# Pre stage run inside the local-attention loop, with keys and values stored by column modulo 4

## What is computed

```python
h = _L0_tok_ref(x, ...)                      # attention in 8x8 windows
h = h + _L0_attn_ref(_layernorm(h), ...)     # local attention: the stage of the change
h = h + _L0_ffn_ref(_layernorm(h), ...)      # routed experts
h = h + _L1_attn_ref(_layernorm(h), ...)     # linear attention with decay
h = h + _L1_ffn_ref(_layernorm(h), ...)      # binary weights behind a gate

def local_mask(seq_len, window_size=7):      # queries see keys at most 3 rows and 3 columns away
    ok_row = jnp.abs(row[:, None] - row[None, :]) <= half
    ok_col = jnp.abs(col[:, None] - col[None, :]) <= half
    return ok_row & ok_col
qkv = (x @ W_qkv.T).reshape(Bb, Nn, 3, NUM_HEADS, HEAD_DIM)
attn = jnp.einsum('bhqd,bhkd->bhqk', q, k) * (scale * temperature[0])
attn = jax.nn.softmax(jnp.where(mask, attn, -jnp.inf), axis=-1)
out = jnp.einsum('bhqk,bhkd->bhqd', attn, v) @ W_proj.T + b_proj
```

## Time and profile before

| | us |
|---|---|
| median of 3 runs | 1976.49 |
| lowest, highest | 1973.61, 1978.38 |
| the profiled execution's own time | 1986.12 |
| its span, first to last instruction | 1984.3 |
| PE busy in the span | 1697.9 (86%) |
| DVE, ACT, POOL busy | 1182.7, 975.5, 422.9 |
| mean granted TensorE clock (share of full speed) | 0.955 |

### The profile page before, as it was taken

How to read it: one execution, slowest core, us unless ns; L and a number is a source line. 1 busy time by engine, 2 the same in 40 slices (tenths; PEclk the granted TensorE clock), 3 DMA queues, 4 the chain that set the end, 5 groups by cost and what they waited for, 6 DMA issues and landing times.

```text
span 1984.3 us, 94332 instructions
## 1 busy us (share of the span) xinstructions
PE 1697.9 (86%) x35690; PEld 1234.3 (62%) x35690; DVE 1182.7 (60%) x3445; ACT 975.5 (49%) x1765; POOL 422.9 (21%) x477
## 2 busy tenths in 40 slices
PE   5999999956568888888888779999999999999996
PEld 3566666644457666666667556666666666666663
DVE  2565656567624444444444467777777777777762
ACT  2344444423312222222222227777777777777776
POOL 2100000034322332323323222222222222222210
PEclk9899999978979999999999969999999999999998
DMA  3100000125533333333333212333333333333332
GB/s 106 36 11 13 11 11 13 32 57 104 102 86 93 92 96 94 93 96 91 97 96 92 63 33 74 79 79 79 79 79 79 79 79 79 79 79 79 79 78 57
DMA packets 254173, 141.71 MB, mean 71 GB/s; under 512 B 181314, under 2 KB 218050, under 8 KB 253858
## 3 DMA queue, kind: packets, MB, share of 16 engines
q1 hardware_dynamic: 254114, 140.88, 29.5%
HBM read 63.56 MB, written 18.42 MB: 41 GB/s over the span
## 4 chain that ended last, share of the span: by engine, by line
issue 33%; PE 29%; SPq 26%; ACT 6%; DVE 2%; DMA 2%; POOL 1%; ACTq 0%; DVEq 0%; POOLq 0%
SPq L402 13%; PE ps_D L805 8%; SPq L391 4%; ACT prob L1060 3%; PE ps_AV L822 3%; SPq L373 2%; PE ps_J L859 2%; PE ps_J L911 2%; PE ps_OT L929 2%; PE ps_J L879 2%; SPq L428 1%; PE ps_J L937 1%; PE ps_OT L954 1%; SPq L394 1%; PE ps_OT L953 1%
## 5 line engine op out<-in xcount | busy, mean ns | idle before, releaser
L1060 ACT ACTIVATE prob<-ps_D 128x1024 bf16<-128x1024 f32 x448 | 443.6, 1022 | 83.6 <-PE ps_D L805 83.2
L1231 DVE TENSOR_REDUCE m_sb<-ps_D 128x4 f32<-128x400 f32 x256 | 135.4, 571 | 207.7 <-PE ps_D L708 192.1
L1048 ACT ACTIVATE prob<-ps_D 100x512 f32<-100x512 f32 x256 | 139.0, 595 | 216.8 <-PE ps_D L730 216.8
L493 POOL TENSOR_TENSOR tile_a<-q_st,q_mask 128x1024 f32<-128x1024 f32 x64 | 123.3, 1927 | 407.5 <-DMA q_st<-q_d 369.5
L730 PE MATMUL ps_D<-tile_a,key_patch 64*100 64x128 f32 x2048 | 176.7, 288 | 0.0
L726 PE MATMUL ps_D<-mT,key_rows 64*100 64x128 bf16 x1024 | 129.3, 224 | 51.0 <-ACT mT L1037 32.2
L1184 DVE TENSOR_REDUCE top<-ps_D 128x8 f32<-128x512 f32 x128 | 79.5, 684 | 152.5 <-PE ps_D L582 152.5
L805 PE MATMUL ps_D<-tile_b,w_parts 128*128 128x256 bf16 x1024 | 155.5, 275 | 15.5 <-ACT prob L1060 9.6
L805 PE MATMUL ps_D<-tile_a,w_parts 128*128 128x256 bf16 x1024 | 156.1, 276 | 14.2 <-ACT prob L1060 9.6
L730 PEld LDWEIGHTS ps_D<-tile_a,key_patch 64*100 64x100 f32 x2048 | 146.8, 166 | 0.0
L805 PEld LDWEIGHTS ps_D<-tile_a,w_parts 128*128 128x128 bf16 x1024 | 88.5, 100 | 60.3 <-issue 47.8
(11 more groups left out here) (174 smaller groups left out, 3880.9 us busy)
## 6 DMA issues: line engine op xcount, KB each, us to landing
tile_b<-v_d SPq DMA_DIRECT2D x640, 40.0 KB
tile_a<-xg SPq DMA_DIRECT2D x384, 64.0 KB, 2.0
tile_b<-xg SPq DMA_DIRECT2D x384, 64.0 KB, 2.0
key_st<-k_d SPq DMA_DIRECT2D x64, 175.0 KB, 3.0
key_st<-k_d SPq DMA_DIRECT2D x64, 167.0 KB, 3.1
w_exp<-experts SPq DMA_DIRECT2D x64, 129.0 KB, 2.3
k_d<-kpad SPq DMA_DIRECT2D x32, 140.0 KB, 2.3
xin<-in_x SPq DMA_DIRECT2D x32, 128.0 KB, 2.3
```

The costliest lines, as they stand in the source:

```text
L493: gp.tensor_tensor(q_block[:, par, :].rearrange("c (p h q) -> c p h q", h=NH, q=NQ), q_st[:, :].rearrange("c (p a q) -> c p a q", a=1, q=N ...
L1048: act.activation(prob1[0:NKL, 2 * g + x, :], s_loc[x][0:NKL, :], ACT.Exp).then_inc(T2["exp_done"], 1)
L1060: act.activation(sgn[:, k % 4, :], unit(k, par)[:, :], ACT.Sign).then_inc(BN["sign"], 1)
L1231: dve.tensor_reduce(m_sb[:, C * x + HOT[x] + 4 * g:C * x + HOT[x] + 4 * g + 4], m_loc[x][:, 0:4 * NKL].rearrange("p (u n) -> p u n", u=4), ...
```

## The change

The pre stage loses its own loop. It now works by strips of 256 tokens (64 instead of 32 turns of half the size), and its strip `m = i + 5` (`LEAD = 5`) is worked in the same turn as local strip `i`, on PE, ACT and DVE; moments and normalization (DVE, POOL) are for `i + 6`. Five strips of it run alone ahead of the loop. SP has one loop, too: in the turn of strip `i` it loads the edge rows of `i`, waits until pre strip `i + 2` is stored, loads keys and queries of `i + 1`, loads the values of `i`, and stores pre strip `i + 3`.

In `k_d` and `v_d` a row is now four groups of 18 columns, one for each column modulo 4 (`NC = 18`, `ROW = 72`; before, 70 columns in order). The columns of one offset for the 16 patches then lie together in `v_d`, so values come in four transfers of 30, 30, 20 and 20 partitions with 4096 bytes each. The keys of a patch have a new order (`key_order`), applied in the host's tables and in two copies on POOL instead of one.

```diff
             def store_rows(b, s, m, par):
-                sp.wait_ge(L["k_sb"], times(i + 1))
+                sp.wait_ge(L["k_sb"], times(m + 1))
...
-                for y in range(2):
-                    dst = v_d[bass.ds(b, 1), bass.ds((w * WIN + HALF + y) * PW, 7 * PW), :].rearrange("a n c -> (a n) c")
-                    sp.dma_start(bass.AP(dst.tensor, dst.offset + HALF * C, [[C, W], [2 * PW * C, 4], [1, C]]),
-                                 v_sb[C * y:C * (y + 1), par, :, :]).then_inc(L["stored%d" % par], 16)
+                for t in range(2):
+                    dst = v_d[bass.ds(b, 1), bass.ds((s * QP + HALF + 2 * t) * ROW, 2 * ROW), :].rearrange("a n c -> (a n) c")
+                    sp.dma_start(bass.AP(dst.tensor, dst.offset + C, [[NC * C, 2 * QP], [C, W // QP], [1, C]]),
+                                 v_sb[:, par, t, :]).then_inc(L["stored%d" % par], 16)
...
+            def values_in(b, s, i, par):
                 sp.wait_ge(T2["av_done"], credited((i - 1) * 2))
                 settle(sp)
-                for r in range(KS):
-                    src = v_d[bass.ds(b, 1), bass.ds((s * QP + r) * PW, PW), :].rearrange("a n c -> (a n) c")
-                    sp.dma_start(v_patch[r * KS:(r + 1) * KS, par, :, :], bass.AP(src.tensor, src.offset, [[C, KS], [QP * C, 16], [1, C]])).then_inc(T2["v_in%d" % par], 16)
+                for column, first, steps in ((1, 0, 3), (2, 0, 3), (0, 1, 2), (3, 0, 2)):
+                    src = v_d[bass.ds(b, 1), bass.ds(s * (QP * ROW) + column * NC + first, NC), :].rearrange("a n c -> (a n) c")
+                    sp.dma_start(v_patch[at:at + KS * steps, par, :, :].rearrange("k a c -> k (a c)"),
+                                 bass.AP(src.tensor, src.offset, [[ROW * C, KS], [C, steps], [1, (W // QP) * C]])).then_inc(T2["v_in%d" % par], 16)
...
+            def strip_io(b, s, pair, par):
+                i = b * STRIPS + s
+                edge_in(s, i, par)
+                stored(b * (STRIPS // 2) + pair + 1, par)
+                keys_in(b, s + 1, i + 1)
+                values_in(b, s, i, par)
+                store_rows(b, s + 3, i + 3, 1 - par)
```

(of `strip_io` the cases at the ends are left out). POOL and PE in a strip:

```diff
-                gp.tensor_copy(key_patch[:, par, :].rearrange("c (p r w) -> c p r w", p=8, r=KS), patches(key_st)).then_inc(T2["k_patch"], 1)
+                keys = key_patch[:, par, :].rearrange("c (p n) -> c p n", p=8)
+                gp.tensor_copy(keys[:, :, 0:6 * KS].rearrange("c p (b r w) -> c p b r w", b=2, r=KS), patches(key_st, NC, NC, 3)).then_inc(T2["k_patch"], 1)
+                gp.tensor_copy(keys[:, :, 6 * KS:10 * KS].rearrange("c p (b r w) -> c p b r w", b=2, r=KS), patches(key_st, 1, 3 * NC - 1, 2)).then_inc(T2["k_patch"], 1)
...
                 scores(j, par, 0)
+                if not last:
+                    peak(*after(j, par), 0)
+                if m is not None:
+                    pre_turn(m)
                 if not first:
-                    project(i - 1)
+                    project(i - 1, min(i + LEAD, NS) if isinstance(i, int) else i + LEAD)
+                if m is not None:
+                    pre_values(m, 1 - par)
                 scores(j, par, 1)
                 if not last:
-                    peak(*after(j, par), 0)
+                    peak(*after(j, par), 1)
                 values(j, par, 0)
+                if m is not None:
+                    pre_keys(m, 1 - par, i)
                 if not last:
-                    peak(*after(j, par), 1)
+                    turn_maxima(i + 1, made(j, par))
                 values(j, par, 1)
-                if not last:
-                    turn_maxima(i + 1)
```

More of the change, by code:

```diff
@@ L43, in head_rows, with key_order @@
     return r // 32, r % 32 // HD, r % HD
+def key_order():
+    order = []
+    for b, steps in ((1, (0, 1, 2)), (2, (0, 1, 2)), (0, (1, 2)), (3, (0, 1))):
+        order += [r * KS + QP * step + b - 1 for r in range(KS) for step in steps]
+    return order
 def shape_tables():
@@ L286, in strips_ahead, with ahead, made @@
             strip(0, 1)
-            with eng.Fori(1, NSTRIP // 2 - 1) as j:
+            full = (NSTRIP - LEAD - 1) // 2
+            with eng.Fori(1, full) as j:
                 strip(j, 0)
                 strip(j, 1)
-            strip(NSTRIP // 2 - 1, 0)
-            strip(NSTRIP // 2 - 1, 1)
+            for j in range(full, NSTRIP // 2):
+                strip(j, 0)
+                strip(j, 1)
+        def ahead(j, par):
+            i = j * 2 + par
+            m = i + LEAD
+            return m if not isinstance(i, int) or m < NSTRIP else None
+        def made(j, par):
+            i = j * 2 + par
+            return min(i + LEAD + 1, NSTRIP) if isinstance(i, int) else i + LEAD + 1
         def pairs(eng, part, end=1):
@@ new lines, in image @@
+            def image(b):
+                with sp.Fori(0, STRIPS // 2 - 2) as pair:
+                    strip_io(b, pair * 2, pair, 0)
+                    strip_io(b, pair * 2 + 1, pair, 1)
+                for pair in (STRIPS // 2 - 2, STRIPS // 2 - 1):
+                    strip_io(b, pair * 2, pair, 0)
+                    strip_io(b, pair * 2 + 1, pair, 1)
+            sp.wait_ge(T1["av_done"], times(NT))
+            store_rows(0, 0, 0, 0)
+            store_rows(0, 1, 1, 1)
+            sp.wait_ge(L["padded"], times(16 * 6 * B))
@@ L409, in _ @@
+            stored(0, 0)
+            stored(0, 1)
+            keys_in(0, 0, 0)
+            store_rows(0, 2, 2, 0)
+            with sp.Fori(0, B - 1) as b:
+                image(b)
+            image(B - 1)
             sp.wait_ge(s_prep, 2)
@@ L1043, in strip, with weights @@
                 i = j * 2 + par
-                for g in range(2):
+                m = ahead(j, par)
+                def weights(g):
                     act.wait_ge(T2["scores"], credited(i * 2 + g + 1))
@@ L1251, in strip @@
                 i = j * 2 + par
+                m = ahead(j, par)
+                nxt = made(j, par)
+                more = not isinstance(nxt, int) or nxt < NS
                 first, last = isinstance(i, int) and i == 0, isinstance(i, int) and i == NS - 1
+                if not last:
+                    maxima(i + 1, 0)
                 if not first:
                     residual(i - 1)
+                if more:
+                    pre_moments(nxt)
                 if not last:
-                    maxima(i + 1, 0)
                     maxima(i + 1, 1)
+                if m is not None:
+                    pre_queries(m, j + 2 + par, 1 - par)
+                if more:
+                    pre_norm(nxt)
                 weigh(i)
```

258 lines of the change are left out of this document (147 added, 111 removed).

## The result

The changed kernel takes **2040.08 us** (median of 4 runs, 2036.62 to 2048.03) against 1977.43 for the kernel before on the same chip (1973.61 to 1981.2). The ratio is 1.0326, with a 95% interval of 1.0305 to 1.0347: slower by 3.3%, where 1919.5 us and a range of 1872 to 1970 had been forecast. The profiled execution took 2038.93 us, its span is 2037.0 (before 1984.3), its mean granted clock 0.924 (before 0.955).

What follows compares the result with a forecast made beforehand. SP's issuing was taken to bound local, a loop of four stores pre. Start -124, intervals +65 and end +2 make -57 us; against the median of 1976.5 that forecast 1919.5 us, range 1872 to 1970.

Steps and rivals of the forecast that it cites:

- Start: Up to the second query load: it comes at 432.7 us instead of 556.65, a gain of 124 us.
- the sum: The forecast's addition of start (-124), 62 intervals between query loads (+65) and end (+2): -57 us.
- Interval on SP: SP's time from keys to keys, now with stores in each strip: 9.98 us against 8.93, +65 us over 62.
- I take the first, since both move ten image rows: SP's value loads: issue taken from the 10x16x64 load's 287 ns, so four at 0.556 us spacing make 2.22 us.
- the dear end: Upper bound for a value load's issue, the costliest shape's 703 ns, giving +1.7 us a strip.
- Rival 2: SP's four value loads: long rows issue slowly; at 703 ns the interval is 11.6 us, 2022 us; chance 0.12.
- One sign that it named: Evidence for slow long rows: the two key loads of 64 rows take 1.35 us together on SP.
- Landing: SP's wait each strip for the last value store to land: 2.2 us, plus 0.4 restart, 62 times.
- the hole behind the edge load: Gap of 1.2 to 1.5 us expected on SP behind each edge load, ended by a v_d store.
- What lies beside it: Other engines' work per strip, covered by SP's 10 us: PE 9.2, POOL 3.7, DVE 5.5, ACT 3.2.
- The wait for mT: PE's wait for the negated maxima, 0.5 us a strip before; hardly any was expected after the change.
- The 9.2 us that PE was to need: PE's strip: 8.6 us busy plus remaining idle and group waits, next bound if SP's cover went.

Runs made afterwards that it cites:

- e9: The changed kernel with value transfers of 32, 32, 16 and 16 partitions, rows contiguous in DRAM (wrong values): 1915.39 us, ratio 0.9682.
- e15: The changed kernel with each value row 256 B behind the last in DRAM, not 18432 B (wrong values): 1913.74 us, ratio 0.967.
- e4: The changed kernel with value loads put ahead of the wait for the stores and of the keys: 2019.68 us, ratio 1.0203.
- e8: The changed kernel with the edge row of strip i+1 issued ahead of the stores of turn i: 2085.41 us, ratio 1.0554.
- e10: The changed kernel with key and value stores issued by ACT and SP's query store moved behind the query load: 1846.21 us, ratio 0.9319.

## Why the prediction was wrong

- **Start: right.** 130 us gained, 124 forecast; the first store went out at 410.1 us where the sum had 414.4.
- **Interval on SP: right in kind, wrong in one term.** SP's issuing set the strip, as said. By the sum's own pieces, from the turn at 716.67: keys to queries 1.70 (forecast 1.55), queries to values 0.71 (0.72), values to key store 4.55 (2.22 + 0.2), key store to first value store 1.87 (1.79), first to second value store 0.97 (0.90), and from there to the next keys 2.35 (2.60). That is 12.15 against 9.98, and 2.13 of the 2.17 lie in the value loads. (This turn is 0.28 us above the mean of 11.87.)
- **The failed step** is "I take the first, since both move ten image rows". The issue taken at 0.287 us measured 0.802, beyond the dear end of 0.703 too; four loads fill 4.10 us where the sum had 2.22. Ten image rows were the wrong likeness. The 96 rows of 4096 B at 347 ns were no nearer, since they too are walked in one step. With the walk taken away, the same sum holds to 0.1 or 0.2 us (e9 9.86, e15 9.81).
- **Rival 2** is what happened (0.12, 2022 us at 703 ns). Its rule, dear from 0.52 us an issue, gave the right side. Its reason, long rows, was wrong: long rows are cheap and 256 B rows dear, if in groups. One sign that it named, the two key loads at 1.35 us together, is not explained by the walk either: their 64 partitions are walked in one step.
- **Landing: right, a little long.** The wait stands where it was put, behind the edge load. The halved store lands 1.94 us after its issue (median of 42 waits), where the 64 KB one took 2.2. So the hole behind the edge load is shorter than the 1.2 to 1.5 us that had been said: 0.62 and 1.04 us behind the two edge loads of the turn shown (716.05 to 716.67, 727.78 to 728.82), with the address work in it. e4 and e8 show the wait from both sides, 20 us and 45. By the rule of the Trainium skill, page "DMA: Bandwidth & Descriptors", section "Anatomy of one DMA", half the bytes do not halve the landing: the trace agrees, and is a little below the 2.08 estimated from it. That section speaks of DMAs that GpSimd issues, which the prediction left out; these stores are issued by SP. The landing in the chain that ended last, from the issue of the second value store of the turn shown:

```profile
726.47 1.94 DMA v_d<-v_sb
```

- **What lies beside it: mostly right.** The wait for mT is gone. PE's busy time, 8.6 forecast, is 8.7 in e9 (389.43 us over 440 / 9.86 strips), and 8.1 in e10. The 9.2 us that PE was to need is too much: e10 runs at 8.64. The edge row as PE's last wait was not foreseen. It cost nothing of its own, since SP, which sets the strip, waited for no engine in that window, only for the landing (19.4 us). With it PE stood idle 2.3 us a strip, and its granted clock fell to 0.88. In e9 it was back at 0.98.
- **Range.** The bounds on the unknown issue were +0 and +1.7 us a strip. The dear one led to 2022 us, but stood outside a range that ended at 1970.

## What to carry to other kernels

Where a queue's issues bound a loop, the price of a transfer there did not follow its bytes or its rows. Before merging transfers, find a row of the same *walk over partitions* in a trace, or put the shape into a running kernel: four shapes cost one run. A merged load that needed two steps over the partitions cost 2.5 times a plain one here (0.80 us for 0.32, e9), so order the data so that one fixed step does it. And what a bound queue has too much of can go to an engine with idle time (here 1.8 us of issues a strip to ACT), as long as nothing that waits stands ahead of a load that others wait for.

## What was not expected of the hardware

- A load is issued on SP in 0.28 to 0.40 us for 8 to 40 partitions in a row at one fixed step in DRAM, with rows of 256 to 4096 B in up to 16 pieces. With the partitions in two steps or three apart it takes 0.67 to 0.87 us.
- That rule does not cover all transfers here. The key loads (0.57 us each), the key store (0.58) and the query store (0.70) have 64 partitions in a row at one step, and are dear all the same. The value stores (0.66) do walk DRAM in two steps, eight groups of 16, but took 0.60 before, in one step of 64. The reason stays open.
- ACT issues the same stores at about SP's price: 617 ns for a value store and 527 for keys in e10, against 662 and 577 on SP in the changed kernel.
- A load hidden behind a landing is free, and moving it "earlier" costs its issue and address work, 0.7 us (e8).
